# The heads pass of a four-layer graph kernel: gathered sum rows and one product moved from VectorE to GpSimd

## The reference

```python
def _L1_gnn_ref(h, W_fc, attn_l, attn_r, W_res, src, dst):
    hh = h.reshape(n, H, D)                      # 12 heads of 64
    ft = jnp.einsum('nhd,ed->nhe', hh, W_fc)
    e = jax.nn.leaky_relu(a1[src] + a2[dst], negative_slope=NEG_SLOPE)
    ...
    alpha = ee / denom[dst]
    agg = jax.ops.segment_sum(alpha[:, :, None] * ft[src], dst, num_segments=n)
    res = jnp.einsum('nhd,ed->nhe', hh, W_res)
    return jax.nn.relu((res + agg).reshape(n, H * D))
...
x = _layernorm(x + _L1_gnn_ref(x, ...), axis=-1)
```

## Time and profile before

| | us |
|---|---|
| median of 3 runs | 4187.57 |
| the profiled execution | 4185.82 |
| its span, first to last instruction | 4184.0 |
| outside the span (difference) | 1.8 |
| heads pass, first instruction of POOL to first of the next stage | 1840.27 to 2248.29 |

### The profile page before, as it was taken

The page is one execution under the profiler, slowest core; times in us unless marked ns, Lnnn a source line. Parts: engine busy times, 40 slices in busy tenths (PEclk is TensorE's granted clock), DMA queues, the critical chain, the costliest instruction groups (busy, mean ns, idle before and its releaser), DMA issues. The chain is left out here.

```text
span 4184.0 us, 64009 instructions
## 1 busy us (share of the span) xinstructions
PE 3690.6 (88%) x21456; PEld 3423.5 (82%) x21456; DVE 2600.0 (62%) x4978; ACT 1181.5 (28%) x1691; POOL 584.2 (14%) x597
## 2 busy tenths in 40 slices
PE   6999999999998881168887899998799998799999
PEld 5999999999995440148885799997699998599999
DVE  4967973276244882749995577775344443477777
ACT  2222232222223441025553222222222222222222
POOL 5520001324310005130003000002200001300000
PEclk9999999999999995589999999999999999999999
DMA  3555665455435881067776444444544444566665
GB/s 99 171 182 183 189 195 163 140 166 183 149 102 163 248 249 45 19 176 246 246 248 227 147 173 172 172 169 176 185 169 171 171 169 146 194 228 229 225 229 180
DMA packets 346284, 742.11 MB, mean 177 GB/s; under 512 B 85045, under 2 KB 137991, under 8 KB 346144
## 3 DMA queue, kind: packets, MB, share of 16 engines
q1 hardware_dynamic: 252656, 502.95, 38.1%
q10 hardware_dynamic: 67584, 154.63, 9.4%
q0 software_dynamic: 25904, 82.71, 6.4%
HBM read 444.88 MB, written 301.21 MB: 178 GB/s over the span
## 5 line engine op out<-in xcount | busy, mean ns | idle before, releaser
L644 DVE TENSOR_TENSOR fr_lo<-fr_turned_ps,fr_hi 128x768 fp32r<-128x768 f32 x158 | 150.5, 952 | 244.8 <-ACT fr_hi L987 235.6
L2097 DVE SCALAR_TENSOR_TENSOR c3a_y<-c3a_prod,dinv,next_const 128x768 f32<-128x768 f32 x79 | 80.4, 1018 | 289.1 <-PE c3a_prod L2251 289.1
L1117 PE MATMUL fr_prod<-fr_w_hi,fr_hi 128*128 128x396 f32 x948 | 256.1, 351 | 0.0
L1117 PE MATMUL fr_prod<-fr_wu_hi,fr_hi 128*128 128x396 f32 x948 | 255.2, 350 | 0.1
L1117 PE MATMUL fr_prod<-fr_w_lo,fr_hi 128*128 128x396 f32 x948 | 248.5, 343 | 0.0
L1117 PE MATMUL fr_prod<-fr_w_hi,fr_lo 128*128 128x396 f32 x948 | 248.3, 343 | 0.0
L1117 PE MATMUL fr_prod<-fr_wu_lo,fr_hi 128*128 128x396 f32 x948 | 248.3, 343 | 0.0
L2251 PE MATMUL c3b_prod<-next_w_hi,c3b_hi 128*128 128x384 f32 x948 | 248.1, 342 | 0.0
L2251 PE MATMUL cv_prod<-next_w_hi,cv_hi 128*128 128x384 f32 x948 | 248.1, 342 | 0.0
L2251 PE MATMUL c3a_prod<-next_w_hi,c3a_hi 128*128 128x384 f32 x948 | 248.0, 342 | 0.0
L1117 PE MATMUL fr_prod<-fr_wu_hi,fr_lo 128*128 128x396 f32 x948 | 247.7, 342 | 0.0
(11 more groups left out here) (480 smaller groups left out, 8633.8 us busy)
## 6 DMA issues: line engine op xcount, KB each, us to landing
fr_ins<-in_x_dram SPq DMA_DIRECT2D x156, 384.0 KB
h<-fr_outs SPq DMA_DIRECT2D x78, 396.0 KB
u<-fr_outs SPq DMA_DIRECT2D x78, 396.0 KB
up_ut<-u SPq DMA_DIRECT2D x78, 396.0 KB
agg<-fr_zrow SPq DMA_DIRECT2D x78, 390.0 KB
hds_agg<-agg SPq DMA_DIRECT2D x78, 390.0 KB
x<-up_x_o ACTq DMA_DIRECT2D x78, 384.0 KB
hds_row<-x SPq DMA_DIRECT2D x78, 384.0 KB
```

What stands on the lines that cost most here:

```text
L644: v.tensor_tensor(lo[:, s2, :, :], turned_ps[:, 0:KC, :], hi[:, s2, :, :].bitcast(F32), ALU.subtract).then_inc(split_done, 1)
L1117: made = nc.tensor.matmul(prods[s2][:, bank, 0:c1 - c0], l[:, s2, s, :], w[:, s, c0:c1], start=(s == 0 and i == 0), stop=(s == KC - 1 and ...
L2097: ec.link(dve, v.scalar_tensor_tensor(y3, p3, g["dinv"][:, bass.ds(t, 1)], c3, ALU.mult, ALU.add))
```

## The change

The heads pass gets its own function, `heads_pass`. What it does in place of the old one:

- `first_layers` computes two more tables of 128 x 79: `has_in` is 1 for a node with an edge from another node, and `in_i` is the node's number, or a number past the table where `has_in` is 0. Five small DVE instructions and one `iota` on GpSimd.
- SP loads only `hds_row`. GpSimd gathers the rows of `agg` with an indirect DMA per tile (`hds_more`), which skips the numbers past the table. A skipped row keeps what an earlier tile left there, and `has_in` multiplies it by 0.
- GpSimd multiplies row by own weights (the old L2053). DVE keeps the own weights (12 columns, now product and sum in one instruction) and the sum (now with `has_in` as a factor).
- DVE's step has the order add(t), own(t+1), shift_of(t-3), end(t-2). GpSimd's has fetch(t+2), scale(t+1). PE transposes the row blocks first and waits for `hds_x` only behind them.
- GpSimd clears the four buffers of `hds_more` at the start of the pass.
- The part of ScalarE stays as it was (root, normalised tile and store in the same order).

```diff
--- before.py
+++ after.py
@@ -155,7 +155,8 @@
-            "own_d": sb("own_d", [P, NT]), "has_own": sb("has_own", [P, NT]),
+            "own_d": sb("own_d", [P, NT]), "has_own": sb("has_own", [P, NT]), "has_in": sb("has_in", [P, NT]),
+            "in_i": sb("in_i", [P, NT], I32),
...
         update_pass(nc, g, u, out2, x1, sc3)
         attention(nc, g, "l1", 12, sc3, 25, 24)
         gather_sum(nc, g, "l1", x1, D, 12, agg)
-        dense_pass(nc, g, "hds", "heads", a, x2, row=x1, agg=agg)
+        heads_pass(nc, g, a, x1, agg, x2)
         for k, dt in (("w_hi", F32R), ("w_lo", F32R)):
...
             nc.gpsimd.memset(g["ones"][:, :], 1.0).then_inc(consts, 1)
             nc.gpsimd.iota(g["iota"][:, :], [[1, P]], base=0, channel_multiplier=0,
                            allow_small_or_imprecise_dtypes=True).then_inc(consts, 1)
+            nc.gpsimd.iota(pt["node"][:, :], [[P, NT]], base=0, channel_multiplier=1,
+                           allow_small_or_imprecise_dtypes=True).then_inc(consts, 1)
             nc.gpsimd.memset(g["eps"][:, :], EPS).then_inc(consts, 1)
             nc.gpsimd.memset(g["last_lane"][:, :], 0.0).then_inc(consts, 1)
-            pool.wait_ge(consts, 5)
+            pool.wait_ge(consts, 6)
...
             link(v.tensor_copy(g["own"][:, :], pa[:, NT:2 * NT]))
             link(v.tensor_scalar(g["own1"][:, :], g["own"][:, :], 1.0, None, ALU.add))
             link(v.tensor_scalar(g["has_own"][:, :], g["own"][:, :], 1.0, None, ALU.min))
+            link(v.tensor_tensor(g["has_in"][:, :], pt["deg"][:, :], g["own1"][:, :], ALU.subtract))
+            link(v.tensor_scalar(g["has_in"][:, :], g["has_in"][:, :], 1.0, None, ALU.min))
+            link(v.tensor_scalar(pt["node_f"][:, :], g["has_in"][:, :], -float(FAR), float(FAR), ALU.mult, ALU.add))
+            link(v.tensor_tensor(pt["node_f"][:, :], pt["node_f"][:, :], pt["node"][:, :], ALU.add))
+            link(v.tensor_copy(g["in_i"][:, :], pt["node_f"][:, :]))
             bg.to(AT_NODE + 1)
             dve.wait_ge(deg_root, 1)
...
+def heads_pass(nc, g, a, x1, agg, x2):
...
+        row, more = sb("row", [P, UNROLL, D]), sb("more", [P, UNROLL, AGG_W])
+        ix = sb("ix", [P, UNROLL], I32)
+        own_w, x, y = sb("own_w", [P, 2, H]), sb("x", [P, 2, D]), sb("y", [P, 2, D])
+        hi = sb("hi", [P, 2, 2 * KC, P])
...
+                if at_least(t, UNROLL):
+                    sp.wait_ge(prod_read, t - UNROLL + 1)
+                sp.dma_start(row[0:rows_of(t), slot, :], tile_rows(x1, t)).then_inc(loaded[slot], 16)
+            over_tiles(sp, step)
+
+        @block.gpsimd
+        def _(pool):
+            nc.gpsimd.memset(w_st[:, :, :], 0.0).then_inc(w_zero, 1)
+            nc.gpsimd.memset(more[:, :, :], 0.0).then_inc(cleared, 1)
+            pool.wait_ge(cleared, 1)
+
+            def fetch(t, slot, turn):
+                if at_least(t, UNROLL):
+                    pool.wait_ge(built, t - UNROLL + 1)
+                nc.gpsimd.tensor_copy(ix[:, slot:slot + 1], g["in_i"][:, bass.ds(t, 1)]).then_inc(indexed, 1)
+                pool.wait_ge(indexed, t + 1)
+                take_wait(nc, g, scrap_p[:, 0:1])
+                nc.gpsimd.indirect_dma_start(more[:, slot, :], None, agg, bass.IndirectOffsetOnAxis(ap=ix[:, slot:slot + 1], axis=0),
+                                             bounds_check=N - 1, oob_is_err=False).then_inc(more_in[slot], 16)
+
+            def scale(t, slot, turn):
+                pool.wait_ge(loaded[slot], turn * 16 + 16)
+                pool.wait_ge(owned, t + 1)
+                if at_least(t, 2):
+                    pool.wait_ge(turned, t - 1)
+                s2 = slot % 2
+                nc.gpsimd.tensor_tensor(x[:, s2, :].rearrange("p (h f) -> p h f", h=H), row[:, slot, :].rearrange("p (h f) -> p h f", h=H),
+                                        own_w[:, s2, :].unsqueeze(2).to_broadcast([P, H, F // H]), ALU.mult).then_inc(scaled, 1)
+
+            def step(t, slot, turn):
+                b = back(t, slot, turn, -2)
+                if live(b[0]):
+                    fetch(*b)
+                b = back(t, slot, turn, -1)
+                if live(b[0]):
+                    scale(*b)
+            fetch(0, 0, 0)
+            fetch(1, 1, 0)
+            scale(0, 0, 0)
+            over_tiles(pool, step)
+
+        @block.vector
+        def _(dve):
+            v = nc.vector
+
+            def own(t, slot, turn):
+                dve.wait_ge(more_in[slot], turn * 16 + 16)
+                if at_least(t, 2):
+                    dve.wait_ge(scaled, t - 1)
+                v.scalar_tensor_tensor(own_w[:, slot % 2, :], more[:, slot, F:F + H], g["has_in"][:, bass.ds(t, 1)],
+                                       g["has_own"][:, bass.ds(t, 1)].to_broadcast([P, H]), ALU.mult, ALU.add).then_inc(owned, 1)
+
+            def add(t, slot, turn):
+                s2 = slot % 2
+                dve.wait_ge(scaled, t + 1)
+                v.scalar_tensor_tensor(x[:, s2, :], more[:, slot, 0:F], g["has_in"][:, bass.ds(t, 1)], x[:, s2, :],
+                                       ALU.mult, ALU.add).then_inc(built, 1)
+
+            def end(t, slot, turn):
+                s2 = slot % 2
+                dve.wait_ge(multiplied, t + 1)
+                if at_least(t, 2):
+                    dve.wait_ge(polished, t - 1)
+                v.scalar_tensor_tensor(y[:, s2, :].rearrange("p (a f) -> p a f", a=2), prods[s2][:, :, 0:HALF], 0.0,
+                                       row[:, slot, :].rearrange("p (a f) -> p a f", a=2), ALU.max, ALU.add).then_inc(prod_read, 1)
+                dve.wait_ge(prod_read, t + 1)
+                v.bn_stats(stats[:, s2, 0, :], y[:, s2, 0:HALF]).then_inc(halved, 1)
+                v.bn_stats(stats[:, s2, 1, :], y[:, s2, HALF:D]).then_inc(halved, 1)
+                dve.wait_ge(halved, t * 2 + 2)
+                v.memset(scrap[:, :], 0.0)
+                v.bn_aggr(mv[:, s2, :], stats[:, s2, :, :].rearrange("p a s -> p (a s)")).then_inc(spread, 1)
+
+            def shift_of(t, slot, turn):
+                s2 = slot % 2
+                dve.wait_ge(rooted, t + 1)
+                v.reciprocal(rstd[:, s2, :], root[:, s2, :]).then_inc(shifted, 1)
+                dve.wait_ge(shifted, t * 2 + 1)
+                v.scalar_tensor_tensor(shift[:, s2, :], mv[:, s2, 0:1], -1.0, rstd[:, s2, :], ALU.mult, ALU.mult).then_inc(shifted, 1)
+
+            def step(t, slot, turn):
+                if live(t):
+                    add(t, slot, turn)
+                b = back(t, slot, turn, -1)
+                if live(b[0]):
+                    own(*b)
+                b = back(t, slot, turn, 3)
+                if at_least(t, 3) and live(b[0]):
+                    shift_of(*b)
+                b = back(t, slot, turn, 2)
+                if at_least(t, 2) and live(b[0]):
+                    end(*b)
+            dve.wait_ge(cleared, 1)
+            own(0, 0, 0)
+            over_tiles(dve, step, 3)
+
...
+        @block.tensor
+        def _(pe):
+            pe.wait_ge(w_in, 64)
+
+            def turn_over(t, slot, turn):
+                if at_least(t, 1):
+                    pe.wait_ge(hi_done, t)
+                pe.wait_ge(loaded[slot], turn * 16 + 16)
+                for s in range(KC):
+                    nc.tensor.transpose(turned_ps[:, KC + s, :], row[:, slot, s * P:(s + 1) * P], g["ident"][:, :])
+                pe.wait_ge(built, t + 1)
+                for s in range(KC):
+                    made = nc.tensor.transpose(turned_ps[:, s, :], x[:, slot % 2, s * P:(s + 1) * P], g["ident"][:, :])
+                made.then_inc(turned, 1)
+
+            def multiply(t, slot, turn):
+                s2 = slot % 2
+                pe.wait_ge(hi_done, t + 1)
+                if at_least(t, 2):
+                    pe.wait_ge(prod_read, t - 1)
+                for s in range(KC):
+                    o = prods[s2][:, s // 3, (s % 3) * P:(s % 3 + 1) * P]
+                    nc.tensor.matmul(o, hi[:, s2, s, :], w_st[:, 0, :], start=True, stop=False)
+                    made = nc.tensor.matmul(o, hi[:, s2, KC + s, :], w_st[:, 1, :], start=False, stop=True)
+                made.then_inc(multiplied, 1)
+
+            def step(t, slot, turn):
+                if live(t):
+                    turn_over(t, slot, turn)
+                b = back(t, slot, turn, 1)
+                if at_least(t, 1) and live(b[0]):
+                    multiply(*b)
+            over_tiles(pe, step, 1)
 
 
 def dense_pass(nc, g, tag, kind, a, out, scores=None, row=None, agg=None, res=None, weights=None, bias=None):
```

More of the change, by code:

```diff
@@ L283, in prep_tiles @@
                 ("is_last", [NC, P], F32), ("end_r", [NC, P], F32), ("val", [NC, P], F32), ("carry_r", [NC, 1], F32),
-                ("tmp_c", [P, NC], F32), ("deg", [P, NT], F32), ("sq", [P, NT], F32),
+                ("tmp_c", [P, NC], F32), ("deg", [P, NT], F32), ("sq", [P, NT], F32), ("node", [P, NT], F32), ("node_f", [P, NT], F32),
```

(4 more changed lines are left out.)

65 lines of the change are left out of this document (added).

## The result

The changed kernel takes 4122.44 us (4120.27 to 4123.81) against 4189.57 (4187.2 to 4192.62) for the kernel before in the same session, 67 us less by these medians. The measured ratio is 0.9847, 95% interval [0.9835, 0.9858]; the two medians alone give 0.9840. I had said 14 us less. What I called my case did not come; rival 3 did, GpSimd hidden behind TensorE (4132 us, 13%).

The account below looks back on a forecast made before the run. DVE bounded the old pass at 4.80 us a tile; POOL was to bound the new one at 4.6: -15.8 us over 79 tiles, +1 start, +0.5 node tables, so -14, to 4173.5 us; range 4130 to 4262.

Parts of the forecast that it names:

- my case: Heads pass: POOL sets the step at 4.4 to 4.85 us a tile, 4155 to 4190 us; chance 50%.
- rival 3: Heads pass: POOL is hidden, PE bounds at 4.03 to 4.1 us a tile, -55 us, about 4132 us; chance 13%.
- TensorE's own step: Heads pass: PE's step without its wait for the sum, 4.80 - 0.77 = 4.03 us, the bound if POOL were free.
- The one-column sum: In POOL's gather preparation: waits for the end of DVE's sum, about 1.20 us after the product's end.
- the transposes' order: PE's six row-block transposes before the wait shorten sum to product by about 0.64 us, worth nothing while PE has slack.
- VectorE's own 3.86: Heads pass: DVE's step after losing the product, 4.80 - 0.99 + 0.05 = 3.86 us a tile.
- POOL becomes the bound with 4.6 us a tile: Heads pass: POOL's product 1.8 plus fetch 2.7, plus 0.1 for the loop's turn, sets the step.
- Product: POOL's multiplication of row by own weights on 128x768: taken as 1.8 us, bounds 0.84 and 2.15.
- Fetch: POOL's gather with its preparation, held up by DVE's sum: 2.5 to 2.9 us a tile, taken as 2.7.
- The turn of the loop: Added to POOL's step: 0.1 us a tile, from 0.34 us every fourth tile, as DVE pays.
- The traffic: Heads pass DMAs: falls by 79 x about 300 KB, worth nothing, with DMAs 71% busy and nobody waiting long.
- Rival 1: Heads pass: POOL's product holds DVE's small factor in a self-feeding rhythm, 5.7 us a step, +71, 4259 us; chance 20%.

## Why the prediction was wrong

**What held.** TensorE's own step is 3.98, where I had worked out 4.03. The sum with a column takes 1.01 as in the earlier trace rows. The one-column sum is held by VectorE's sum and ends with it in 52 of 79 steps, as in the earlier trace rows, and VectorE's read of the product from PSUM holds nothing, as in the earlier trace rows. The other stages moved by about 1 us, and the transposes' order was worth nothing. VectorE's own 3.86 never bounded; it was too high by about 0.2, since with less work for TensorE VectorE still stands 11.9 us in 53 tiles in front of its sum at that very step.

**The step that failed is "POOL becomes the bound with 4.6 us a tile".** It was the sum of two unknown sizes, both taken too high, and 0.6 us above a second bound, so that the error changed the case:

- Product: I took 1.8 between 0.84 and 2.15, measured 1.464. The value that I had worked out and passed over, two reads in turn (1.50), came within 3%: (1464 - 190) / 768 = 1.66 ns an element, about twice the 0.85 of one stream. The extra products agree: 837 ns for 384 columns is 1.68, 300 for 64 is 1.72. The size is as if the write cost nothing of its own; no run takes reads and write apart. -0.34 us.
- Fetch: I took 2.7 between 2.5 and 2.9, measured 2.35 from the product's end (1856.45) to the next start. The one-column sum ended 1.10 after it, not 1.20; the own weights (1857.42 to 1857.64) fell on the end of the one-column sum (1857.55) and into the 0.15 behind it, so they held nothing; and the gap behind the DMA was 0.03 where I allowed up to 0.31. -0.35. My 2.7 is nearly what the 384-column run shows (2.83), where the hold falls on the index copy and the 0.54 in front of the DMA is paid openly.
- The turn of the loop: with less work for TensorE GpSimd's steps repeat 3.82, 3.83, 3.82, 3.94, so every fourth is 0.12 longer, 0.03 in the mean and not 0.1.

1.46 + 2.35 + 0.03 is 3.84 (the four steps just named give 3.85), under TensorE's 3.98. From there on rival 3's arithmetic holds, (3.98 - 4.82) x 78 = -65. Of its two conditions, the product "near 1.3" was nearly met, and "DVE's sum doesn't hold up the fetch" wasn't needed: it does hold it up, but the hold covers 0.39 of the 0.54 us of preparation that has to be spent anyway. Even that rival's 4132 was 10 us too long, as it took 4.1 for TensorE's step and not 3.98; a step under the 4.03 that I had worked out was left out of my range.

**The traffic** I priced at nothing because nobody waited for DMAs at 4.80 us a tile. At 3.98 that no longer holds: with whole rows the step is 4.14 and GpSimd waits for row tiles. What is hidden has to be asked again at the new step.

**Rival 1** has a true mechanism (the run with whole rows) and a wrong account of when it decides. It needs the own weights to release the product in each step; in the changed kernel it is mostly the end of POOL's gather, and the product starts 1.38 us after own in the median, when the factor has long passed. My chance of 20% was for its repeating by itself, which no run with an early load showed.

The Trainium skill was used twice. From its figure for an addition of 2048 elements (GPSIMD Engine Reference, section 3.1) I had an estimate of 1.8 us for the product; 1.464 was measured for this multiplication of 768, and the measurement decides. Its rule that the two engines exclude each other for the whole instruction, whoever is first (SBUF — State Buffer, Who interferes with whom), agrees with the runs also in the direction that the trace before didn't show: VectorE's factor took 1.46 us for 0.16 with whole rows.

## What to carry to other kernels

- When work moves to an idle engine, work out that engine's step and the next engine's. Where they are within the spread of an unknown duration, the forecast is of two cases, and each deserves its weight: mine had 0.6 us of margin made of two guesses.
- Bound an unknown instruction by its streams: operands times the one-stream rate was within 3% here, in three widths of one operation. Between bounds, ask what kind of work each one stands for; the middle stands for none.
- A hold-up between engines costs only what it doesn't overlap. Look at what the held engine would have done in that time, and at which instruction releases the long one.

## What the runs showed of the hardware

- A GpSimd multiplication of two SBUF operands takes 1.66 to 1.72 ns an element over 0.19 us (64, 384 and 768 columns: 300, 837 and 1464 ns). For 768 columns VectorE takes 0.96 us.
- The exclusion works both ways, each time to the end of the other's instruction: VectorE's one-column factor 1.46 us for 0.16 with whole rows; its sum 1.57 for 1.02 behind GpSimd's extra 384 columns; GpSimd's one-column sum 0.89 for 0.19 in the changed kernel.
- A gather on GpSimd is held too: 1.20 to 1.64 us in 23 of 79 steps of the changed kernel, each beside VectorE's sum, where 1.07 is the median.
- A gather's 0.53 to 0.61 us before it starts run while the one-column sum ahead of it is held (then 0.15 remain), but not while the index copy is (0.53 remain in the run with 384 extra columns).
